# Two heads of eight groups transposed on VectorE and placed through a scratch in device memory, in a fused two-layer graph attention kernel

## The reference

```python
# layer 0: multi-head attention, H = 8 heads of HD = 32, masked by adj == 0
h = relu(layernorm(x))
Q, K, V = (proj(W, b) for ...)                       # each (16, 8, 1024, 32)
scores = einsum('bhnd,bhmd->bhnm', Q, K) * HD**-0.5
attn = softmax(where(adj == 0, -inf, scores))
x = x + einsum('bhnm,bhmd->bhnd', attn, V) @ Wo.T + bo
# layer 1: four kinds of edges, one score each
h = relu(layernorm(x))
e_k = leaky_relu(einsum('bid,bjd->bij', h * a_k, h))  # k = 0..3
scores = e_{adj-1} where adj is 1..4, else -9e15
x = x + einsum('bij,bjd->bid', softmax(scores), h)
```

## Time and profile before

| | us |
|---|---|
| median of 3 runs | 3792.05 |
| lowest, highest | 3787.47, 3802.44 |
| span of the profiled execution | 3783.3 |
| PE busy | 3454.1 (91%) |
| DVE busy | 2850.7 (75%) |
| ACT busy | 2464.4 (65%) |
| POOL busy | 1125.2 (30%) |
| DMA queue q1, share of 16 engines | 27.0% |

### The profile page before, as it was taken

One profiled execution on the slowest core, in us unless ns is written; L12 is line 12 of the kernel. 1 busy time (PEld: TensorE's weight loads), 2 busy tenths in 40 slices (PEclk: granted clock), 3 DMA queues, 4 the chain that ended last, 5 costly groups with the idle time before them and its releaser, 6 DMA issues.

```text
span 3783.3 us, 97534 instructions
## 1 busy us (share of the span) xinstructions
PE 3454.1 (91%) x34096; PEld 2916.1 (77%) x34096; DVE 2850.7 (75%) x5622; ACT 2464.4 (65%) x4548; POOL 1125.2 (30%) x568
## 2 busy tenths in 40 slices
PE   5889999899998999999899998999989999998975
PEld 4678778787787878778787787877878787787864
DVE  4777778787787878878777787878778787887752
ACT  4775767657676676766757676666766757676541
POOL 2232423323232232423323232232422324233212
PEclk8999999999999999999999999999999999999988
DMA  4141412314132141412414132141321414123101
GB/s 120 51 113 54 128 36 81 93 58 122 40 103 72 59 121 55 112 53 67 107 54 128 40 100 75 54 125 49 110 57 56 122 54 128 40 86 89 37 27 44
DMA packets 166740, 294.99 MB, mean 78 GB/s; under 512 B 25536, under 2 KB 75968, under 8 KB 166080
## 3 DMA queue, kind: packets, MB, share of 16 engines
q1 hardware_dynamic: 166080, 286.63, 27.0%
HBM read 169.09 MB, written 16.78 MB: 49 GB/s over the span
## 4 chain that ended last, share of the span: by engine, by line
PE 61%; issue 11%; ACT 10%; SPq 7%; DVE 7%; DMA 2%; POOL 0%; DVEq 0%; ACTq 0%; POOLq 0%
PE pT L1082 15%; PE pG L1017 13%; PE pG L1095 11%; PE pG L1152 8%; PE ps L1070 7%; SPq L250 6%; ACT sm L490 4%; PE pT L1143 3%; PE pG L1051 3%; DMA adj_half<-in_adj_dram 2%; ACT pt L501 2%; DVE sm L754 1%; DVE pt L766 1%; PE pG L1108 1%; ACT sm L546 1%
## 5 line engine op out<-in xcount | busy, mean ns | idle before, releaser
L754 DVE CUSTOM_DVE_ANT_0 sm<-ps,bias 128x1024 f32<-128x1024 f32 x1024 | 1244.1, 1215 | 20.6 <-issue 17.0
L1082 PE MATMUL pT<-ident,sm 128*128 128x128 f32 x8192 | 1099.7, 276 | 127.0 <-ACT pt L501 108.9
L1082 PEld LDWEIGHTS pT<-ident,sm 128*128 128x128 f32 x8192 | 946.5, 141 | 345.0 <-ACT sm L490 140.4
L490 ACT ACTIVATE sm<-sm,mn 128x1024 f32<-128x1024 f32 x1024 | 1180.5, 1153 | 48.5 <-DVE mn L754 48.0
L501 ACT COPY pt<-pT 128x512 f32<-128x512 f32 x1024 | 596.3, 582 | 592.6 <-PE pT L1082 592.4
L766 DVE COPY pt<-pT 128x512 f32<-128x512 f32 x1024 | 703.0, 687 | 287.1 <-PE pT L1082 281.4
L417 POOL TENSOR_SCALAR gbias<-adj_half 128x512 bf16<-128x512 int32 x256 | 505.2, 1973 | 1324.3 <-DVE mn L865 1030.1
L1070 PE MATMUL ps<-ks,qs 96*128 96x512 f32 x2048 | 760.9, 453 | 76.7 <-DVE mn L754 64.1
L400 POOL TENSOR_SCALAR bias<-adj_half 128x512 bf16<-128x512 int32 x256 | 492.5, 1924 | 785.5 <-DMA adj_half<-in_adj_dram 712.0
L1095 PE MATMUL pG<-pt,v 128*32 128x128 f32 x16384 | 530.7, 283 | 27.5 <-DVE x L889 18.5
L1095 PEld LDWEIGHTS pG<-pt,v 128*32 128x32 f32 x16384 | 455.1, 114 | 87.9 <-issue 39.3
(11 more groups left out here) (104 smaller groups left out, 3328.1 us busy)
## 6 DMA issues: line engine op xcount, KB each, us to landing
adj_half<-in_adj_dram SPq DMA_DIRECT2D x512, 256.0 KB, 2.9
ks<-parts SPq DMA_DIRECT2D x384, 128.0 KB, 2.4
qs<-parts SPq DMA_DIRECT2D x384, 128.0 KB, 2.6
x<-in_x_dram SPq DMA_DIRECT2D x16, 1024.0 KB, 5.6
out_dram<-x SPq DMA_DIRECT2D x128, 128.0 KB, 2.6
x<-in_x_dram SPq DMA_DIRECT2D x32, 256.0 KB, 3.5
rb<-in_x_dram SPq DMA_DIRECT2D x16, 256.0 KB, 3.2
sq<-in_x_dram SPq DMA_DIRECT2D x16, 256.0 KB, 3.3
```

The source lines that it names most:

```text
L490: nc.scalar.activation(sm[:, ring(t), :], sm[:, ring(t), :], ACT.Exp, scale=-1.0, bias=mn[:, t:t + 1], accum_out=den[:, t:t + 1]).then_inc ...
L754: nc.vector.tensor_tensor_reduce(out=sm[:, ring(t), :], in0=ps[t % 2][:, :], in1=bias[:, node, :], scale=1.0, scalar=3e38, op0=ALU.add, op ...
L1082: last = nc.tensor.transpose(pT[c][:, j * P:(j + 1) * P], sm[:, ring(t), m * P:(m + 1) * P], ident[:, :])
```

## The change

In groups 2 to 9 of every element (`SWAPPED`) the tiles of the heads 0 and 1 (`TURNED`, 16 of 64 tiles) are no longer transposed by PE nor copied out of PSUM:

- DVE transposes the 32x32 blocks of such a tile within SBUF, 128x1024 elements in one instruction (`turn`), into `turned`.
- When both tiles of a group are turned, SP writes `turned` to a scratch `bounce` in device memory with four DMAs of 256 KB, one per 32 partitions, in rows of 1 KB. It waits for them, waits for the value product of the group before, and loads the whole (1 MB, 8 KB per partition) into places 0 and 1 of `pt` with one DMA (`swap_blocks`).
- The value product of these groups waits for that load (`swapped`) and stands ahead of the transposes of slot 4g+6, two slots later than before. It reads the turned tiles in four pieces of 32 columns, 1 KB apart.
- The other two tiles of these groups (heads 2 and 3) are transposed by PE as before; ACT now copies both halves of them.
- `turned` lies over the weights of q and k. These are copied to the unused 32 partitions of `ks` once at the start (`park`), and back once per element (`restore`, four DMAs of 256 KB); PE waits for them in slot 47.
- Parts of the edges move by a slot: the sum of an edge block, its result, the order of its exponential; block 6 is kept in `spare`, over `parts`. The rows of the softmax factors and the statistics of the next element's front shift by one to three slots. The loads of x are placed elsewhere in SP's order.

```diff
+SWAPPED = tuple(range(2, 10))
+BATCH = 4 * 16
+TURNED = tuple(HG * g + h for g in SWAPPED for h in range(2))
+PLAIN = tuple(t for t in range(TILES) if t not in TURNED)
...
     for g in range(1, GROUPS - 1):
-        behind[HG * g + HG].append(("av", g))
+        if g in SWAPPED:
+            ahead[HG * g + HG + 2].append(("av", g))
+        else:
+            behind[HG * g + HG].append(("av", g))
...
+            def swap_blocks(b, g):
+
+                sp.wait_ge(turn_made, len(TURNED) * b + turned_before(HG * g + 2))
+                settle(sp)
+                half, n = g % 2, SWAPPED.index(g)
+                for a in range(4):
+                    sp.dma_start(bounce[half, :, :, :, a, :].rearrange("c j h w -> j h c w"),
+                                 turned[HD * a:HD * (a + 1), :, :, :, :].rearrange("p h c m j -> p h c (m j)")
+                                 ).then_inc(bounced, 16)
+                sp.wait_ge(bounced, BATCH * (len(SWAPPED) * b + n + 1))
+                settle(sp)
+                sp.wait_ge(av, GROUPS * b + g)
+                settle(sp)
+                sp.dma_start(pt[:, 0:2, :, :].rearrange("p h m n -> p (h m n)"),
+                             bounce[half].rearrange("c j h a w -> (c j) (h a w)")).then_inc(swapped, 16)
...
-                for t in range(4):
-                    edge_adj(o, t, base)
+                edge_adj(o, 0, base)
+                edge_adj(o, 1, base)
+                swap_blocks(b, 2)
+                swap_blocks(b, 3)
+                edge_adj(o, 2, base)
+                swap_blocks(b, 4)
+                edge_adj(o, 3, base)
+                swap_blocks(b, 5)
                 store(o, 0)
                 edge_adj(o, 4, base)
+                swap_blocks(b, 6)
                 store(o, 1)
                 edge_adj(o, 5, base)
+                if later:
+                    load_xf(b + 1, 3)
+                swap_blocks(b, 7)
                 store(o, 2)
                 edge_adj(o, 6, base)
                 store(o, 3)
                 if later:
                     front_load(b)
+                swap_blocks(b, 8)
+                if later:
                     sp.wait_ge(y_out, 16 * (NT * o + 4))
                     settle(sp)
                     front_load_x1(b)
                 edge_adj(o, 7, base)
+                swap_blocks(b, 9)
...
             for t in range(2, NT):
                 sp.wait_ge(most_made, t)
                 settle(sp)
                 load_adj(0, t, t)
                 if t == 2:
                     second_stacks(0, 1)
+                if t > 2:
+                    swap_blocks(0, t - 1)
...
+                if t // HG in SWAPPED:
+                    act.wait_ge(tr[1], len(PLAIN) * b + plain_before(t) + 1)
+                    nc.scalar.copy(pt[:, place(t), NT // 2:, :], pT[1][:, :].rearrange("p (m n) -> p m n", n=P)
+                                   ).then_inc(pt_made[1], 1)
...
+            def turn(b, t, first):
+
+                dve.wait_ge(exped, TILES * b + t + 1)
+                if t == TURNED[0] and first:
+                    dve.wait_ge(parked, BATCH)
+                if t % HG == 0 and (t > TURNED[0] or not first):
+                    dve.wait_ge(bounced, BATCH * (len(SWAPPED) * b + SWAPPED.index(t // HG)))
+                settle(dve)
+                nc.vector.transpose(turned[:, t % HG, :, :, :].rearrange("p c m j -> p m c j"),
+                                    sm[:, ring(t), :].rearrange("p (m c j) -> p m c j", m=NT, c=4)
+                                    ).then_inc(turn_made, 1)
...
-                    copy(b, s, not earlier)
+                    if s in TURNED:
+                        turn(b, s, not earlier)
+                    elif s // HG not in SWAPPED:
+                        copy(b, s, not earlier)
...
+                if g in SWAPPED:
+                    pe.wait_ge(swapped, 16 * (len(SWAPPED) * b + SWAPPED.index(g) + 1))
...
                     for h in range(HG):
                         o = (HG * hg + h) * HD
-                        last = nc.tensor.matmul(pG[i][HD * h:HD * (h + 1), 0:P], v[:, m, o:o + HD],
-                                                pt[:, place(HG * g + h), m, :], start=(m == 0), stop=(m == NT - 1))
+                        if HG * g + h in TURNED:
+                            moving = swap[:, h, :, m, :]
+                        else:
+                            moving = pt[:, place(HG * g + h), m, :]
```

More of the change, by code:

```diff
@@ L63, in background @@
         for t in range(NT):
-            behind[EDGE + 4 + 4 * t].append(("sum", t))
+            behind[EDGE + (5 if t in LATE or t == SPARED else 4) + 4 * t].append(("sum", t))
     if later:
@@ L315, in stage @@
                     mask_adj(b + 1, 0, base)
+                    restore(b)
                 store(o, 5)
@@ L593, in stage @@
                         edge_copy(o, NT - 1)
+                    edge = (s - EDGE - 3) // 4 if earlier and EDGE + 3 <= s < EDGE + 3 + 4 * NT and s % 4 == 0 else None
+                    if edge in LATE:
+                        edge_exp(o, edge)
                     if s + 1 < TILES:
@@ new lines, in stage @@
+                    for t in range(NT):
+                        if earlier and s == EDGE + (5 if t in LATE else 4) + 4 * t:
+                            pe.wait_ge(lpt[0], NT * o + t + 1)
+                            pe.wait_ge(lpt[1], NT * o + t + 1)
+                    if s not in TURNED:
+                        transposes(b, s, not earlier)
+                    for t in range(NT - 1):
+                        if earlier and s == EDGE + (7 if t in LATE else 6) + 4 * t:
+                            edge_values(o, t, pG[bank("sum", t)], (1, 2, 3) if t == SPARED else (2, 3))
@@ new lines, in stage @@
+                    for kind, n in behind[s]:
+                        product(kind, n, len(PLAIN) * b + plain_before(s + 1))
+                    if earlier and EDGE + 3 <= s < EDGE + 3 + 4 * NT and s % HG == 0:
+                        pe.wait_ge(pt_made[0], len(PLAIN) * b + plain_before(s + 1))
+                        pe.wait_ge(pt_made[1], len(PLAIN) * b + plain_before(s + 1))
+                        edge_transposes(o, (s - EDGE - 3) // 4)
+                    for t in range(NT - 1):
+                        if earlier and s == EDGE + (6 if t in LATE else 5) + 4 * t and t != SPARED:
+                            edge_values(o, t, pG[bank("sum", t)], (1,))
```

168 lines of the change are left out of this document (106 added, 62 removed).

## The result

The changed kernel takes 3841.97 us (median of 4 runs, 3830.1 to 3854.0), the kernel before 3792.87 on the same chip. The ratio is 1.0131 with an interval of 1.0104 to 1.0158: 1.3% slower, where 3737 was forecast. The profiled execution has a span of 3839.9 us against 3783.3, and a mean granted clock of 0.952 against 0.974. The trace of the kernel before is of an execution at the fast end, 8.8 us under its median, so up to a microsecond or so per element can lie between two traces without a cause in the kernels.

What follows compares the result with a forecast made beforehand. PE was taken to bound groups 4 to 9 of the 15 elements with edges. Gains of 4.7 us per element, x 15 = 70, less 15 for element 0, net -55, gave 3737 us; range 3650 to 3865.

Steps and rivals of the forecast that it cites:

- Groups 2 and 3: Before the edges begin, PE not the bound: gain between 0 and 0.87 us each, taken as 0.4, in all 0.8.
- the path: Edge half's end to the waiting product, through device memory: 15.0 us, with write 7.0 and read 5.6; break-even 16.7.
- the turn: DVE's transpose of one tile within SBUF: taken as 1.22 us, bounds 0.69 and 2.4; DVE then not the bound.
- Groups 4 to 7: Groups with edges, bound by PE: 13.6 us each instead of 14.48, a gain of 0.85 each, 3.4 per element.
- Groups 8 and 9 with tile 41: Gain 1.3 us per element, with 0.2 less each for queued x loads; tile 41 waiting for group 9's product costs 0.8.
- Element 0: The element without edges: +4 us for longer groups and +11 for adjacency loads behind SP's waits and the read, +15.
- the loop (4): Element 0's chain over two groups, path included: 19.8 us, 9.9 per group against 9.40, +0.5 x 8 = 4.
- ACT's copies, zero: ACT loses two PSUM copies per group and gains two of 0.582 us: no cost, since it has cover.
- The strided operand: Value product reading turned tiles in strided pieces: taken as zero cost, at most 0.9 us.
- (B): Rival: path short enough, 13.6 us, that PE is the bound again; kernel at 3659 us; chance 0.17.
- (C): Rival: path exceeds 16.7 us, so PE waits longer than the transposes took; 3890 us with an 18.5 path; chance 0.23.
- (E): Rival: PE's waits let its clock fall; 3810 us if every second group lost 1.8; chance 0.07.

Runs made afterwards that it cites:

- this run: The changed kernel, unaltered, run again on the chip of three follow-up runs: 3854.53 us, ratio 1.0158 to the kernel before.
- e1: The changed kernel with groups 4 to 9 swapped instead of 2 to 9: 3773.12 us, ratio 0.9935 to the kernel before.
- e4: The changed kernel with both legs of the path through memory cut to 32 KB, for timing alone: 3788.94 us, ratio 0.9964.
- e14: As e4, with each turn also cut to 128x128, an eighth of its elements, for timing alone: 3742.67 us, ratio 0.9868.
- e9: The changed kernel with element 0's adjacency loads put ahead of the swaps on SP's queue: 3859.94 us, ratio 1.0174.
- e8: The changed kernel with each turn issued twice, 1.24 us more of VectorE per turned tile: 4041.19 us, ratio 1.0639.

## Why the prediction was wrong

Its terms per element, in the order of the sum, against the means of before and after:

- **Groups 2 and 3, -0.8: the step that failed, and the largest miss.** Measured +2.6 (slots 4 to 15), which over 14 elements is 47 of the 116 us by which the sum missed this run. The prediction had seen that waits between PE, ACT and DVE set the end there, and still bounded the effect at "between 0 and 0.87 each", excluding a loss. e1 against this run says nearly the same: with groups 2 and 3 as before, slots 4 to 43 are 2.3 us shorter. Of the 2.6, the path has 1.5 (e4) and the turn 0.3 (e14 against e4), both measured; for the other 0.8 there are two candidates, ScalarE's order and the clock, not told apart.
- **Groups 4 to 7, -3.4:** measured -1.7 (slots 15 to 31), another 24 us. Groups 5 to 7, in stretches where PE had no gap before, give -3.5, more than the 2.6 forecast for them. The price of PE's work was right (12.74 us), and so was the path: the read is issued 7.0 us behind the writes, as forecast, and lands after 5.0, not 5.6. Group 4, whose slots 15 to 19 had gaps already, loses 1.8: PE waits there 1.7 us for the norm and 1.8 for the exponential of the edge block. In e1 neither wait stands there and these slots gain 2.0, but the next ones lose 2.5, the entry price. So either way the first stretch behind where the turned groups begin lost, and the sum had no term for it. SP's rows of the changed kernel:

```profile
1965.85 3.48 SPq L335 DMA_DIRECT2D bounce<-turned  x4
1972.87 0.34 SPq L342 DMA_DIRECT2D pt<-bounce  x1
```

- **Groups 8 and 9 with tile 41, -1.3 + 0.8 = -0.5:** measured +1.4 (slots 31 to 43), 27 us. Group 8 loses 0.75, behind the norm's wait again; group 9 gives 1.4; slots 39 to 43 lose 2.0. Tile 41's price stood in the sum; the statistics ahead of tile 40's copy didn't, though the diff moves them.
- **Element 0, +15:** measured +30. All of the 15 was the path and what queues behind it, and e4 gives 12.7 for that; how it divides between the loop (4) and the adjacency loads (11) isn't shown, but SP's order had hardly a part in it (e9). The turn was in the sum only as a link of the loop; that it holds up the masks behind it costs 16.4. (The rest of the 116: 15 us here, 7 in the last element, less 4 behind slot 43.)
- **The turn:** forecast 1.22, measured 1.240, and the next mask starts another 0.17 to 0.19 late. VectorE's busy time per group was forecast at 10.75 and is 10.77. But "not the bound" was read as "free": e8 shows 0.64 us of span for each us added.
- **Not named at all:** the norm's wait, 30 times 1.7 us, and the wait for the edge's exponential, 14 times 1.8 us.
- **ACT's copies, zero:** true for the busy time (26.15 and 26.06 in slots 4 to 15), not for the order. The strided operand: the mean matmul went from 283 to 288 ns, at most 15 us in all, with a lower clock in it.

Of the rivals, (B) named a short path and priced it at 3659; e4 had the short path and measured 3789. (C), a path over 16.7 us, did not occur, though the slower side did. (E), the clock, is real in part: the mean granted clock fell from 1.00 to 0.92 in slots 4 to 15 and from 0.95 to 0.86 in slots 15 to 19, but in slots 19 to 43 it stays at 0.99 to 1.00. That PE's new waits made it fall is argued, not shown. The time came out in the range and on the side that was given 0.30; that it lies in the range is luck, since the causes found are not those that the upper part of the range stood for.

The Trainium skill, "DMA: Bandwidth & Descriptors", section "Anatomy of one DMA", would give an estimate of 4.4 us for each leg, by its fit for the other issuing path. The trace has 5.0 for the read and 7.0 for the write, so it doesn't agree here, least for the leg that is four DMAs.

## What to carry to other kernels

Taking work from the busiest engine paid here where that engine had no gap (slots 19 to 31: 44.0 us to 40.5), and where a chain of several engines set the end it mostly cost (slots 4 to 19: 47.3 to 51.7). Price a change stretch by stretch, and in a stretch that a chain sets, let the bounds reach below zero. An engine at 73% is not free: ask what stands in its queue behind the added work, and who waits for that. A change also moves things in stretches that it does not touch: before a gain is credited to an edit, look where in the trace it stands. In e1 all of it stood at the return of the loop, and no edit had been aimed at that.
